# V's stored weights ahead of the prepared pieces in SyncE's queue of DMAs

## What is computed

```python
x = x + attention(layernorm(x))            # 16 heads of 128, tanh cap 50, causal, a sigmoid gate per head
x = x + experts_by_token_id(layernorm(x))  # 4 experts; Wg = Wu = Wd = ctx_2048[e], 512 x 512
x = x + moe(layernorm(x))                  # shared expert of 704, and the best 2 of 8 experts of 352
```

```python
qkv = (x @ w_qkv).reshape(b, n, 3, H, DH).transpose(2, 0, 3, 1, 4)
sim = tanh(q @ k.T * SCALE / 50) * 50      # causal mask, softmax over keys
out = softmax(sim) @ v * sigmoid(x @ w_gates)
out = out @ w_out
```

## Time and profile before

| | us |
|---|---|
| median of 3 runs | 1728.98 (1726.3 to 1730.95) |
| the profiled execution | 1726.06 |
| its span, first to last instruction | 1724.3 |
| PE busy | 1669.6 (97%) |
| DVE, POOL, ACT busy | 889.6, 713.6, 596.8 |
| POOL on the pieces' low parts (x45) | 120.5 |

### The profile page before, as it was taken

The page is one execution under the profiler, slowest core; times in us unless marked ns, Lnnn a source line. Parts: engine busy times, 40 slices in busy tenths (PEclk is TensorE's granted clock), DMA queues, the critical chain, the costliest instruction groups (busy, mean ns, idle before and its releaser), DMA issues.

```text
span 1724.3 us, 25547 instructions
## 1 busy us (share of the span) xinstructions
PE 1669.6 (97%) x8672; PEld 1440.8 (84%) x8673; DVE 889.6 (52%) x1518; ACT 596.8 (35%) x1048; POOL 713.6 (41%) x610
## 2 busy tenths in 40 slices
PE   7999999999999999999999999999999999999996
PEld 5888888888888888888888877888998998999995
DVE  4777656676665766566666664352525222222221
ACT  4444443444344334343433433332121112232331
POOL 4666554564554564455555531112002411334342
PEclk9999999999999999999999999997989999999998
DMA  8776456677677677667677755534300014687843
GB/s 286 292 277 244 141 202 206 214 289 268 207 254 260 215 279 264 230 228 271 239 254 303 264 220 187 195 125 151 136 13 20 19 19 165 181 275 217 253 85 43
DMA packets 94974, 344.43 MB, mean 200 GB/s; under 512 B 15165, under 2 KB 15204, under 8 KB 89252
## 3 DMA queue, kind: packets, MB, share of 16 engines
q1 hardware_dynamic: 80836, 305.46, 48.9%
q0 software_dynamic: 14048, 37.79, 9.3%
HBM read 221.64 MB, written 121.58 MB: 199 GB/s over the span
## 4 chain that ended last, share of the span: by engine, by line
PE 62%; POOL 16%; issue 15%; DMA 4%; DVE 2%; ACT 1%; SPq 0%; POOLq 0%; ACTq 0%; DVEq 0%
PE bank L306 19%; PE bank L308 18%; PE bank L307 18%; POOL pre_split L520 5%; POOL key_sums L571 3%; POOL probs L561 3%; DMA store<-wv_parts 3%; POOL key_sums L569 2%; POOL key_sums L567 2%; PE bank L1526 2%; PE bank L1499 2%; PE bank L1583 1%; PE bank L1401 1%; PE bank L1572 1%; DMA rows<-xs 0%
## 5 line engine op out<-in xcount | busy, mean ns | idle before, releaser
L561 POOL TENSOR_TENSOR probs<-probs,causal 128x256 f32<-128x256 f32 x126 | 90.7, 740 | 415.4 <-ACT probs L745 415.4
L306 PE MATMUL bank<-store,wqk 128*128 128x512 f32 x512 | 202.2, 395 | 0.0
L308 PE MATMUL bank<-store,wqk 128*128 128x512 f32 x512 | 202.1, 395 | 0.0
L307 PE MATMUL bank<-store,wqk 128*128 128x512 f32 x512 | 202.0, 395 | 0.0
L1014 DVE SCALAR_TENSOR_TENSOR resid<-bank,factor,resid 128x512 f32<-128x512 f32 x256 | 189.1, 740 | 10.4 <-PE bank L308 10.3
L1008 DVE TENSOR_TENSOR q_lo<-bank,q_hi 128x512 fp32r<-128x512 f32 x64 | 44.3, 692 | 196.7 <-ACT q_hi L785 196.7
L840 ACT ACTIVATE act_sb<-bank 128x352 f32<-128x352 f32 (+1 forms) x93 | 44.4, 496 | 287.5 <-PE bank L308 287.5
L743 ACT ACTIVATE probs<-bank 128x512 f32<-128x512 f32 x189 | 85.8, 527 | 158.0 <-PE bank L308 158.0
L1180 DVE TENSOR_TENSOR aT_lo<-bank,aT_hi 64x128 fp32r<-64x128 f32 (+3 forms) x148 | 56.5, 422 | 128.2 <-ACT aT_hi L831 122.3
L1022 DVE TENSOR_TENSOR p_lo<-probs,p_hi 128x1280 fp32r<-128x1280 f32 x63 | 120.6, 1914 | 2.2
L520 POOL TENSOR_TENSOR pre_split<-pre_raw,pre_split 128x1152 fp32r<-128x1152 f32 x45 | 120.5, 2678 | 0.0
(11 more groups left out here) (255 smaller groups left out, 4382.3 us busy)
## 6 DMA issues: line engine op xcount, KB each, us to landing
pre_parts<-pre_split SPq DMA_DIRECT2D x45, 1152.0 KB, 5.6
wqk<-wqk_parts SPq DMA_DIRECT2D x96, 512.0 KB, 3.4
pre_raw<-pre SPq DMA_DIRECT2D x45, 576.0 KB, 6.5
store<-wv_parts SPq DMA_DIRECT2D x12, 2048.0 KB, 10.7
wo<-wo_parts SPq DMA_DIRECT2D x48, 512.0 KB, 6.1
expert_w<-pre_parts SPq DMA_DIRECT2D x8, 2816.0 KB, 11.3
wqk_parts<-wqk SPq DMA_DIRECT2D x16, 1024.0 KB, 5.6
expert_w<-pre_parts SPq DMA_DIRECT2D x8, 1536.0 KB, 8.5
```

Source lines behind the costliest of these rows:

```text
L306: nc.tensor.matmul(out_ap, a_hi, b_hi, start=first, stop=False)
L307: nc.tensor.matmul(out_ap, a_hi, b_lo, start=False, stop=False)
L308: return nc.tensor.matmul(out_ap, a_lo, b_hi, start=False, stop=last)
L561: nc.gpsimd.tensor_tensor(diagonal, diagonal, causal[:, :, :], ALU.mult).then_inc(S["masked"], 1)
```

## The change

In SP's loop, the block that handles a piece (its first load, its store, the load of the next) is moved from in front of the block that handles V's weights to behind it. Nothing else is different. In turns 20, 24 and so on to 56 (10 turns) the order becomes: V's weights, store of the piece, load of the next. In turn 16 V's weights go ahead of the load of the first piece. Turn 12 has no piece, and the first 16 turns no other overlap.

```diff
-                j = u - PRE_SLOT
-                if j == -1:
-                    load_pre(0)
-                if 0 <= j < PRE_JOBS:
-                    sp.wait_ge(S["pre_lo"], j + 1)
-                    sp.dma_start(pre_parts[:, :, j * PRE_JOB:(j + 1) * PRE_JOB], plain(pre_split[:, :, :])).then_inc(S["pre_stored"], 16)
-                    if j + 1 < PRE_JOBS:
-                        load_pre(j + 1)
                 g = u // TB + 1
                 if u % TB == 0 and GROUPS <= g < U // TB:
                     if g == GROUPS:
@@
                     store_wv(g)
                     if g + 1 < GROUPS:
                         sp.dma_start(wv_raw[:, :, :], wv_in[g + 1]).then_inc(S["wv_loaded"], 16)
+                j = u - PRE_SLOT
+                if j == -1:
+                    load_pre(0)
+                if 0 <= j < PRE_JOBS:
+                    sp.wait_ge(S["pre_lo"], j + 1)
+                    sp.dma_start(pre_parts[:, :, j * PRE_JOB:(j + 1) * PRE_JOB], plain(pre_split[:, :, :])).then_inc(S["pre_stored"], 16)
+                    if j + 1 < PRE_JOBS:
+                        load_pre(j + 1)
```

## The result

The changed kernel takes 1735.33 us (median of 20 runs, 1724.0 to 1744.86), the kernel before beside it 1728.0 (20 runs). The ratio is 1.004, with a 95% interval from 1.0022 to 1.0058: 7 us more. The profiled execution has a span of 1728.7 us against 1724.3; the stretch that the change touches, from V's end in turn 16 to V's end in turn 56, grew by more than that, from 633.9 (280.18 to 914.06) to 644.5 us (279.70 to 924.17). The rest of the program, in which nothing changed, was 6.2 us shorter in this one execution, and the clock accounts for it: outside the stretch the granted clock stood at half for 61 us in the trace before and for 49 in the changed one, which is 6 us of work. Of the changed kernel's 20 runs the five at a mean granted clock of 0.985 to 0.989 took 1724.0 to 1733.2 us, and the fifteen at 0.979 to 0.983 took 1733.6 to 1744.9, so the medians are the better measure.

What follows compares the result with a forecast made beforehand. PE was taken as the bound, idle 8.8 of 712 us. Losing its waits for V's weights (-10.1) and gaining a wait for DVE (+11.9) gave +1.8 us, so 1730.8 against 1728.98; range 1722.5 to 1737.5.

Steps and rivals of the forecast that it cites:

- Part 1: V's weights, loaded 2.5 us earlier in turn 20, land before PE asks; all 7 waits go: -10.1 us.
- Part 2: On SP's queue the piece's store and next load come behind V's 2048 KB, so the raw piece lands later: X 12.8 us.
- X: Time from V's end to the landing of the raw piece, 3776 KB in all; taken as 12.8 us, bounds 11.9 and 13.4.
- instruction packet: Instruction-queue packet holding up one of 16 DMA engines during the transfers; 1.3 us added to X in five turns.
- slow start: V's load, when first, moves 238 GB/s in its first 2 us against 406 when the piece leads: 0.8 us.
- Part 3: Late raw piece delays ACT's copy, k_hi, DVE's k_lo and y_add; PE newly waits 11.9 us in ten turns.
- Part 4: Edits costing nothing: turn 16's first piece load, POOL's low part (1.3 us later with a packet), later wo and wqk weights.
- Rival A: Transfer order on the queue is free, X 11.9 or 13.2 us; -5.4 us in sum, 1723.6; chance 0.22.
- Rival B: Slower: the copy on ACT becomes the bound, X 13.4 us; +7.8 us, 1736.8; chance 0.23.
- Rival C: Transfers share the DMA engines, V's weights and piece land about as late as now; PE unaffected, 1729; chance 0.05.

Runs made afterwards that it cites:

- second execution: The changed kernel, with nothing further changed, run and profiled once more for a second look at the same waits: 1735.85 us in one run.

## Why the prediction was right, and where it was off

It forecast no measurable change, at 1730.8, with 0.25 for slower by over 0.3% and a range that holds the 1735.3. The likeliest case was +1.8 us, and the measured +7 lies 2 us beyond what it called no change: most of the mechanism was right, one term was too small, and the clock was not in it.

**Part 1 was right.** No wait for V's weights is left, and with the other wait out of the way the kernel gained 8 to 16 us, where 10.1 stood; the stretch of turns 16 to 56 got 9.7 us shorter in its profile.

**Part 2 failed in the size of X.** The order of landings was right: 9.4, then the store, then the raw piece. The prediction took 12.8 for a turn without an instruction packet, between bounds of 11.9 and 13.4. In such turns X was 13.7, 13.2 and 13.3 on the mean in the changed kernel's two executions and in the one with the copy moved. So the upper bound, from the turn in which V's load led, was the value to take. The step that was off is "nearer to the turns in which V's load did lead": a mean of two bounds, of which one was measured in another order of the same transfers. With its packets the forecast comes to 13.45 on the mean of ten turns, against 14.0 and 13.6; the second execution's wait of 12.0 us is the forecast's 11.9. The slow start is there, 238 GB/s in the first 2 us of data with V's load in front, the value of turn 12, and 238 to 270 over the ten turns:

```profile
342.00:344.00 2.00, 2.00 (x17) 1.91 (x16) 1.10 (x2) 0.35 (x1) 0.35 (x1) 1.00 0.96 238
```

A second thing was not in the sum: the 16 engines leave V's load one by one. From 348 on the queue already moves packets of the piece (under 8 KB), though the last of V's land at 350.5:

```profile
DMA packets 41, 0.28 MB, mean 284 GB/s; under 512 B 10, under 2 KB 10, under 8 KB 29
```

(That is 348 to 349 us.) What that adds isn't shown, as the kernel before hands over in the same way: from 412 to 413, in its turn 24, the queue moves packets of the piece's load and of V's beside each other (under 8 KB and 16 KB). By these rates and the 406 of the earlier trace rows the slow start is worth some 0.7 us, an estimate, and X without a packet grew from 11.9 by 1.3 to 1.8; where the rest comes from stays open.

**The instruction packets** were given 1.3 us each. The five turns with one had 14.3 on the mean, the five without 13.7: 0.5 rather than 1.3. In the second execution it was 14.1 against 13.2, so 0.9. This term was too large, and partly hid that the other was too small.

**Part 3 was right step by step.** 3.1 us from landing to PE, limits of 12.1 and 12.5. With the measured X its sum is 14.0 x 10 - (6 x 12.1 + 4 x 12.5) = 17.4 us, and PE waited 15.9 and some 0.1 for each restart. -10.1 + 16.9 is +6.8, and with 3.1 for the clock +9.9; this profile's stretch grew by 10.6. For the second execution the same sum is -10.1 + 13.0 + 1.6 = +4.5, and its stretch grew by 5.5. The +7.3 of the medians lies between them.

**Part 4 was right in what it costs.** Behind turn 16 the first piece's copy starts at 290.29, and PE doesn't wait. POOL waits 12.3 us for the copy, in all ten turns, where the prediction had 1.3 in five; PE never waits for POOL.

**Rival A fell.** The same bytes took 14.0 us instead of 11.9 to 13.3 when V's load led. With it falls what was worked out from the Trainium skill ("DMA: Bandwidth & Descriptors", Bandwidth), 11.9 us; the page gives those rates and its fixed cost for DMAs issued from GpSimd, and these are SP's. **Rival B** was what happened: with its instruction packets its X is 14.05 on the mean of ten turns, against 14.0 and 13.6, and its price of +7.8 was nearly met; its place on ACT is shown by the run with the copy moved. **Rival C** fell with the landings.

**Not foreseen:** the clock. By this profile's two stretches it adds 3.1 us, by the second execution's one 1.6. Rival B had no clock in it either, so that its +7.8 lies so near the +7.3 of the medians is in part luck. The waits of the kernel before, 2.1 us at most, were of a length that may bring it and in its profile didn't.

## What to carry to other kernels

A transfer moved to the front of a queue is paid for by those behind it, so look who waits for the last one, and through which chain: here a copy that nobody needed soon stood on ACT in front of one that everybody needed. Moving that copy behind `k_hi` cost nothing, and turned a loss of 0.4% into a gain of 0.7%. When X is to be estimated, take it from a stretch in which the same transfer leads, since the same bytes in the old order landed 1.2 to 1.6 us sooner on the mean (12.4 against 13.6 and 14.0).

## What the runs showed of the hardware

- The order of the same transfers makes a difference: 3776 KB landed in 11.9 to 13.3 us with the 1152 KB store in front and in 12.9 to 15.4 with the 2048 KB load in front. Halving the load's packets changed nothing. Why the load starts slowly stays open.
- Two queues with work at once share the engines by packets and not by bytes: in 2 us one moved 35 packets of 16 KB and the other 30 of 4.6 KB, 0.57 against 0.14 MB. The 2048 KB that were issued first landed in 10.0 us on the mean of eight turns, instead of 9.7 and 9.5 with one queue, and the last of the 1728 KB behind them 13.5 us after V's end, instead of 14.1 and 13.7.
- A wait of PE of 1.7 to 3.2 us in a stretch without other gaps brought 3.4 us at half clock in 5 of 16 cases, and one of 3.4 us or more in all 17. A wait can so cost nearly twice what the waits list shows.
